# Score units of the pairs that run alone: two banks claimed and two masks made ahead of their products

## The reference

```
L0: softmax attention on compressed, normalised q and k   ("mla")
    + experts, top 4 of 8
L1: grouped softmax attention with rotary q and k         ("gqa"), then experts, top 2 of 8
    + sparsemax attention, max(z - tau, 0)                ("spm")
out = x + all of these
```

## Time and profile before

| | |
|---|---|
| time, median of 3 runs | 3134.1 us (3131.94 to 3136.5) |
| the profiled execution: time, span | 3129.51 us, 3127.6 us |
| busy, share of the span | PE 90%, DVE 68%, ACT 52%, POOL 48% |
| mean granted TensorE clock, share of full | 0.956 |
| masks (L524) | 1896 matmuls, 432.9 us busy |

### The profile page before, as it was taken

How to read it: one execution, slowest core, us unless ns; L and a number is a source line. 1 busy time by engine, 2 the same in 40 slices (tenths; PEclk the granted TensorE clock), 3 DMA queues, 4 the chain that set the end, 5 groups by cost and what they waited for, 6 DMA issues and landing times. The chain is left out here.

```text
span 3127.6 us, 61182 instructions
## 1 busy us (share of the span) xinstructions
PE 2809.4 (90%) x20990; PEld 2275.6 (73%) x20990; DVE 2133.4 (68%) x6013; ACT 1615.2 (52%) x3388; POOL 1506.6 (48%) x2213
## 2 busy tenths in 40 slices
PE   5877799999999999978998898998799999999996
PEld 3555478888899889846666666666588888888864
DVE  6878678788788788767777877766644444454565
ACT  3544344444454445545655555655455555555553
POOL 4768743443343354385556666322233333332487
PEclk8878799999999999989999999999899999999998
DMA  3555578788888888422333344210466666665355
GB/s 83 197 208 202 196 262 311 278 286 316 284 290 307 294 286 308 178 40 55 97 99 104 105 107 109 93 69 22 164 213 210 228 213 212 204 241 203 124 97 126
DMA packets 212008, 580.13 MB, mean 185 GB/s; under 512 B 24617, under 2 KB 146417, under 8 KB 167409
## 3 DMA queue, kind: packets, MB, share of 16 engines
q1 hardware_dynamic: 172528, 523.82, 47.7%
q0 software_dynamic: 36864, 51.14, 8.1%
q10 hardware_dynamic: 2304, 1.21, 0.1%
HBM read 450.14 MB, written 125.96 MB: 184 GB/s over the span
## 5 line engine op out<-in xcount | busy, mean ns | idle before, releaser
L1139 POOL TENSOR_TENSOR al<-t,ah 128x512 fp32r<-128x512 f32 x220 | 283.4, 1288 | 875.1 <-ACT ah L1375 875.1
L481 PE MATMUL bank<-xh,gu 128*128 128x256 f32 x3520 | 672.3, 291 | 33.6 <-DVE gc L1654 25.8
L481 PEld LDWEIGHTS bank<-xh,gu 128*128 128x128 f32 x3520 | 512.6, 190 | 57.7 <-issue 55.0
L524 PE MATMUL bank<-masks_bf,ident_bf 128*128 128x128 bf16 x1896 | 432.9, 252 | 133.9 <-DVE st L1840 41.0
L1840 DVE TENSOR_REDUCE st<-bank 128x1 f32<-128x512 f32 (+3 forms) x1024 | 422.1, 481 | 166.1 <-PE bank L542 158.6
L1472 ACT ACTIVATE pt<-bank 128x512 f32<-128x512 f32 (+1 forms) x1152 | 512.0, 540 | 30.2 <-PE bank L545 21.9
L524 PEld LDWEIGHTS bank<-masks_bf,ident_bf 128*128 128x128 bf16 x1896 | 170.3, 99 | 353.6 <-DVE st L1840 95.3
L1480 ACT ACTIVATE oT<-bank 128x512 f32<-128x512 f32 x192 | 114.6, 597 | 602.5 <-PE bank L621 576.5
L542 PE MATMUL bank<-ksT,qsT 128*128 128x512 f32 (+3 forms) x1536 | 410.3, 369 | 5.7 <-DVE top L1838 3.1
L545 PE MATMUL bank<-qaT,ksT 128*128 128x512 f32 (+3 forms) x1536 | 399.6, 372 | 0.0
L481 PE MATMUL bank<-xl,gu 128*128 128x256 f32 x1760 | 351.5, 281 | 0.0
(11 more groups left out here) (250 smaller groups left out, 5216.2 us busy)
## 6 DMA issues: line engine op xcount, KB each, us to landing
gu<-wu_scratch SPq DMA_DIRECT2D x110, 1032.0 KB, 5.2
gu<-wu_scratch SPq DMA_DIRECT2D x110, 1024.0 KB, 7.4
dn<-wd_scratch SPq DMA_DIRECT2D x110, 1024.0 KB, 6.7
xs<-xs_scratch SPq DMA_DIRECT2D x110, 264.0 KB, 4.3
ys_scratch<-yb SPq DMA_DIRECT2D x110, 256.0 KB, 7.0
raw<-in_gu SPq DMA_DIRECT2D x16, 1024.0 KB
wu_scratch<-hi SPq DMA_DIRECT2D x16, 1024.0 KB
wu_scratch<-lo SPq DMA_DIRECT2D x16, 1024.0 KB
```

Of the source, the lines that this page charges most:

```text
L481: mm = pe.matmul(bank[:, TS * h:TS * (h + 1)], gu[:, col:col + P], x[s % 2][:, TS * k:TS * (k + 1)], start=(n == 0), stop=(n == len(terms) ...
L524: return pe.matmul(S.bank((which, G, u))[:, diag:diag + P * len(unit)], ident_bf[:, :], masks_bf[:, side, 0:len(unit), :].rearrange("p n k ...
L1139: pool.tensor_tensor(em["al"][s % 2][:, m, :], em["t"][g % 2][:, :], em["ah"][s % 2][:, m, :].bitcast(F32), ALU.subtract).then_inc(al_read ...
```

## The change

In `scores`, for calls that make their masks first, the six units are taken two by two: both banks are claimed (both waits), both masks are issued, the mask with fewer columns first, and then the products of both units in their old order. Calls with `bare` or `masks_last` keep their order. Nothing is computed otherwise, and the number of matmuls is the same.

```diff
-                    for u in units:
+                    def claim_unit(u):
                         name = (which, G, u)
                         S.add(name, "dve" if which == "q" else "act")
                         if S.former[name]:
                             pe.wait_ge(*S.former[name])
-                        bank = S.bank(name)
+                    def products(u):
+                        bank = S.bank((which, G, u))
                         unit = (Q_UNITS if which == "q" else K_UNITS)[u]
-                        if not bare and not masks_last:
-                            mask(u, True)
                         for n, (j, blk, first, width) in enumerate(unit):
...
-                        if not masks_last:
-                            mm.then_inc(s_full, 1)
+                        return mm
+                    if bare or masks_last:
...
+                    else:
+                        for i in range(0, len(units), 2):
+                            two = units[i:i + 2]
+                            for u in two:
+                                claim_unit(u)
+                            for u in sorted(two, key=lambda u: len((Q_UNITS if which == "q" else K_UNITS)[u])):
+                                mask(u, True)
+                            for u in two:
+                                products(u).then_inc(s_full, 1)
```

More of the change, by code:

```diff
@@ L546, in scores @@
                                                mem["qaT"][:, T - width:T], start=begin, stop=end, skip_group_check=True)
-                        if not masks_last:
-                            mm.then_inc(s_full, 1)
+                        return mm
+                    if bare or masks_last:
+                        for u in units:
+                            claim_unit(u)
+                            mm = products(u)
+                            if not masks_last:
+                                mm.then_inc(s_full, 1)
+                    else:
+                        for i in range(0, len(units), 2):
+                            two = units[i:i + 2]
+                            for u in two:
+                                claim_unit(u)
+                            for u in sorted(two, key=lambda u: len((Q_UNITS if which == "q" else K_UNITS)[u])):
+                                mask(u, True)
+                            for u in two:
+                                products(u).then_inc(s_full, 1)
                     if masks_last:
```

## The result

The changed kernel takes 3203.22 us (median of 4 runs, 3191.27 to 3209.64) beside 3135.3 (3131.94 to 3139.42) for the kernel before on the same chip: a ratio of 1.0222, interval 1.0195 to 1.0249. The prediction was 3187 us and slower by 1.7%: the measured time is inside its range of 3148 to 3212 and 1 us above the forecast's own 3172 to 3202. It is 8 us more than that of the medians, 67.9. Lines of the changed kernel stand lower: L542 and L545 are now L544 and L547, L621 is L638, L1840 is L1857, L1472 is L1489.

The account below looks back on a forecast made before the run. TensorE's own sequence was taken to set the middle's end. Middle 44, end 3 and start 6 sum to 53 us on the profiled 3129.5, so 3182.5; the median is 4.6 above: 3187 us, range 3148 to 3212.

Parts of the forecast that it names:

- Place and mechanism: Units 4 and 5 both wait for the later bank; q call ends 0.33 us later, k call 0.31.
- Group size: Work of units 4 and 5 left behind the later bank: 0.67 us in a q call, 0.57 in a k call.
- The gate: When bank 1 comes free after the call's start: 1.97 us in a q call, 1.77 in a k call.
- fewer turns: TensorE's turns between mask and product: 0.19 us saved per q call, 0.24 per k call; at most 53 us.
- The loss of a step: Per step 0.33 + 0.31 + 0.05 x 52/79 = 0.67 us; middle 53 us, +44 after absorption.
- this mechanism: In some 15 steps the next q call waits for ScalarE's key copies, shifting about 0.2 us less than TensorE: -3 us.
- The start: Steps before 410 us and from 1310 to 1410: loss between 0 and 19 us, a third taken, 6.
- The end: From 2957 to 3005 us, 4 steps lose 3 us; from 3005 on, 0.
- TensorE stays the faster one: From 3005 us: TensorE's steps of 8.43 us plus 0.65 stay below GpSimd's 9.43, so the loss there is 0.
- The waits cost nothing: Rival: bank 1 is free by 1.2 us, savings stay, up to 53 us go; 3105 us with half; chance 0.06.
- The lateness is absorbed: Rival: 27 of 79 middle steps absorb it and the start gives nothing; about 3163 us, chance 0.24.
- The idle stretches lower the clock: Rival: added gaps drop the middle's clock from 0.97 to 0.92, adding 36 us; 3223 us, chance 0.10.

Follow-up runs that it names:

- last_alone: The change with units 0 to 3 in twos but units 4 and 5 each alone: 3138.39 us beside 3129.19 for the kernel before, ratio 1.0032.
- claims_only: The change with both banks claimed first but each mask directly ahead of its own products: 3192.86 us beside 3129.19 for the kernel before, ratio 1.021.
- one_wait: The change with one wait for the later bank where the same engine empties both: 3181.8 us beside 3129.19 for the kernel before, ratio 1.0185.
- two_waits: The kernel before, plus an already met wait for the previous unit's bank ahead of each odd unit: 3135.24 us beside 3127.46, ratio 1.0026.
- k_only: The change in k calls alone, q calls in single units: 3161.73 us beside 3130.22 for the kernel before, ratio 1.0098.
- q_only: The change in q calls alone, k calls in single units: 3171.49 us beside 3129.19 for the kernel before, ratio 1.0131.

## Why the prediction was right, point by point

**Place and mechanism: right.** The loss is the third pair's group behind the later bank. `last_alone` takes it away and `claims_only` has all of it, so it lies in the claims of units 4 and 5, not in the masks.

**Group size: right to 0.01.** 0.67 and 0.57 us were predicted behind the gate, 0.66 and 0.57 stand in the timeline. So was the saving ahead of the gate, which was said to be lost in the wait.

**The gate: 0.08 to 0.13 too early.** The prediction put the third pair at 1.97 + 0.05 in a q call and at 1.77 in a k call; the calls shown have 2.10 and 1.90. `one_wait` and `two_waits` give the missing 0.09, the instruction that a second wait adds, for which the prediction had nothing. The listing of the change shows three waits where six stood, but six are issued still. In the k call there is a further 0.04: ScalarE's first exponential starts at 0.670 in place of 0.630, so the copy of the outputs covers the second mask only in part. The step "fewer turns" was right but on the wrong side of the gate.

**The loss of a step: mis-sized, the middle right by luck.** By the medians a q call grew 0.46 and a k call 0.43 us: 0.89 to a step, where 0.67 was predicted. The middle has 88 steps, so 79 us. Summed over its calls one by one, they grew some 68 us; the other 11 are missing in calls that grew less than the median, as those would that had waited long before. The stage grew 49.1. The prediction took 53 for 79 steps, 9 of it absorbed, or 0.56 a step; measured is 49.1 / 88 = 0.56. What it had too small was both the loss and the absorption, and they cancel. Of the signs that it named, `outputs` stood 0.45 us later and not 0.33 to 0.38, the k call took 2.47 and not 2.33, and the masks' waits for VectorE's `st` came to 92.8 us, not over 100.

**Where 19 us went: between the k call and the next q call.** The stretches from the end of a k call (the turn of the outputs, L452) to the next q call shrank by some 19 us in all, 18.3 of it behind the k calls of p = 2, 4 and 6. In one step of p = 4, before:

```profile
1589.23 0.60 PE L452 MATMUL bank<-ident,oT 128*128 128x128 f32 x4
...
1592.01 1.53 PE L576 MATMUL bank<-w_gqa,xT 128*128 128x384 f32 x4 [0.87 <-ACT ksT L1459]
...
1594.25 0.22 PE L524 MATMUL bank<-masks_bf,ident_bf 128*128 128x128 bf16 x1
```

and after:

```profile
1626.91 0.60 PE L452 MATMUL bank<-ident,oT 128*128 128x128 f32 x4
...
1628.74 1.53 PE L593 MATMUL bank<-w_gqa,xT 128*128 128x384 f32 x4
...
1630.97 0.33 PE L524 MATMUL bank<-masks_bf,ident_bf 128*128 128x128 bf16 x2
```

The stretch is 5.02 us before and 4.06 after, as the wait of 0.87 for ScalarE's key copies is gone. In steps p = 2 the same holds of the waits for VectorE's `xb_gqa`: of 4.3 us in 12 pieces over the middle 1.3 in 6 are left. The prediction had this mechanism with 15 steps and 0.2 us each; there are 33 such steps (11 sequences, three each), and they take 0.55 each. `k_only` shows the same: its calls grew 31 us in the middle, the stage 18. `q_only`'s grew 38.7, the stage 36.7.

**The start: 6 predicted, 16.5 measured.** Here the q and k calls grew 16.7 us in 21 steps, and the stage by as much. A third of the full rate was an estimate without a row behind it. It is not settled why: `q_only`'s calls grew 14.5 us there and the stage 0.4, `k_only`'s 8.1 and the stage 13.5, `one_wait`'s 10.2 and the stage 2.9. Single steps of this stage move by several us from kernel to kernel as GpSimd's and ScalarE's other work falls. `two_waits` lengthened the start by 4 us, so the second wait is not enough to explain it. Nor does the clock, which is 0.77 here and 0.80 before: `last_alone`, at 0.78, has a start as short as the kernel before.

**The end: 3 predicted, 10.7 measured.** "TensorE stays the faster one" is the claim that fell. GpSimd's steps were 9.43 us apart and TensorE's 8.43; with 0.9 more and a slower clock in places, GpSimd waits for TensorE again. GpSimd's first operation of three steps after:

```profile
3073.62 0.29 POOL L1191 CAST qst<-qk 128x128 fp32r<-128x128 f32 x1 [2.89 <-PE bank L452]
...
3094.43 0.29 POOL L1191 CAST qst<-qk 128x128 fp32r<-128x128 f32 x1 [0.69 <-PE bank L452]
...
3114.57 0.29 POOL L1191 CAST qst<-qk 128x128 fp32r<-128x128 f32 x1 [0.30 <-PE bank L452]
```

Before, no wait of GpSimd for L452 stands among the waits from 3005 us on. TensorE's margin of 1.0 us was read from one step, and it was as small as the loss. The clock goes with the rest. From the start of this stage to 3105 us the kernel before ran at 1.00 throughout; the changed kernel has 13.7 us at half of it, in several pieces, and a mean of 0.96 up to 3180 us. In `claims_only`, with calls nearly as long, the clock stayed at 1.00 up to 3170 us and the end grew 4.8 us in place of 10.7. The clock is not all: the end of `one_wait` grew 8.5 us at 0.99. One step of the end, TensorE, after:

```profile
3106.64 0.33 PE L524 MATMUL bank<-masks_bf,ident_bf 128*128 128x128 bf16 x2 [0.84 <-DVE top L1855]
...
3107.55 2.34 PE L638 MATMUL bank<-pt,V 128*17 128x512 f32 x16
```

The products with V take 2.34 us in place of 1.27, and the granted clock in them is 0.50, the lower of TensorE's two levels, behind a wait of 0.84 us (windows, columns as above):

```profile
3107.50:3109.80 2.30, 2.30 (x17) 0.82 (x16) 2.06 (x8) 0.00 (x0) 2.00 (x2) 0.50 0.16 24
```

**The rivals.** "The waits cost nothing" fell: bank 1 comes at 1.97 to 2.02, not 1.2. "The lateness is absorbed" is true of 30 of the middle's 79 us, far from all. "The idle stretches lower the clock" did not hold in the middle, 0.96 before and after; in the start (0.80 to 0.77) and the end (0.95 to 0.93) the mean fell. In the end up to 6 of the 10.7 us go with it, by `claims_only` beside the change; that is one profiled execution of each, and what tipped the clock in one and not in the other stays open.

**The sum.** It was 53 us where the medians moved 67.9. By the profiled executions, cut as here, the start was 10.5 us too small, the end 7.7 and the middle 5 (eight steps that the prediction counted to the start lie in the middle here).

## What to carry to other kernels

A claim moved ahead of other work makes that work wait for the later of the resources: measure when the last one comes free, put behind that gate only what needs it, and count everything else behind it as lost time. What is saved ahead of such a gate is worth nothing here. What brings the gate forward is worth its whole length, less what is moved behind it: the smallest unit first brought the gate of the q call forward by 0.44 us and made the last unit 0.12 longer, and the call gained 0.32. Where two waits for counts of one semaphore stand in a row, keep the larger.

## What the runs showed of the hardware

With one wait ahead of a mask the mask starts 0.058 us after the release (q calls of the kernel before; 0.057 and 0.056 in the q and k calls of `one_wait`). With a second wait on the same semaphore, met long before, it is 0.147 in the q calls and 0.144 in the k calls, in the old order (`two_waits`) as in the new. The unmet wait then has an instruction to itself, which starts 0.040 us after the release, with the mask's load 0.076 behind it. So the cost is not hidden in the time in which TensorE stands waiting; it is added at its end.
